# A decoder's first layer norm: order across tiles, a two-tensor normalise, first loads and value products reordered, one weight's low part on VectorE

## The reference

```python
def _layernorm(x, axis=-1, eps=1e-05):
    m = jnp.mean(x, axis=axis, keepdims=True)
    v = jnp.var(x, axis=axis, keepdims=True)
    return (x - m) / jnp.sqrt(v + eps)
...
x = x + _L0_attn_ref(_layernorm(x, axis=-1), L0_attn_Wq, L0_attn_bq, L0_attn_Wk, L0_attn_bk, L0_attn_Wv, L0_attn_bv, ...)
```

## Time and profile before

| | |
|---|---|
| median of 3 runs | 1648.77 us (1647.23 to 1651.67) |
| the profiled execution | 1647.46 us |
| its span in the trace | 1645.7 us |
| PE busy | 1584.0 us, 96% of the span |
| DVE, ACT, POOL busy | 57%, 45%, 40% |
| chain that ended last | PE 84%, DVE 7%, ACT 4%, issue 4%, POOL 1% |
| granted TensorE clock, mean | 0.996 |

### The profile page before, as it was taken

How to read it: one execution, slowest core, us unless ns; L and a number is a source line. 1 busy time by engine, 2 the same in 40 slices (tenths; PEclk the granted TensorE clock), 3 DMA queues, 4 the chain that set the end, 5 groups by cost and what they waited for, 6 DMA issues and landing times.

```text
span 1645.7 us, 24561 instructions
## 1 busy us (share of the span) xinstructions
PE 1584.0 (96%) x9832; PEld 1347.7 (82%) x9832; DVE 937.4 (57%) x1531; ACT 732.5 (45%) x1231; POOL 665.3 (40%) x483
## 2 busy tenths in 40 slices
PE   7999999989999999989999989998989999999998
PEld 7898666878899998768889976876768888888887
DVE  6555664366545455587758667353666455554554
ACT  3113655322587765666511156333545334353342
POOL 3875542440498873421127634112432422212221
PEclk9999999999999999999999999999999999999999
DMA  4110003123222007200002100110011111111111
GB/s 167 52 65 28 2 2 117 56 84 126 97 89 65 14 1 268 93 1 1 1 8 70 52 27 1 50 39 26 21 33 39 49 61 52 45 50 47 53 57 45
DMA packets 28580, 88.52 MB, mean 54 GB/s; under 512 B 4154, under 2 KB 4282, under 8 KB 28215
## 3 DMA queue, kind: packets, MB, share of 16 engines
q1 hardware_dynamic: 28468, 86.96, 15.3%
HBM read 85.11 MB, written 1.84 MB: 53 GB/s over the span
## 4 chain that ended last, share of the span: by engine, by line
PE 84%; DVE 7%; ACT 4%; issue 4%; POOL 1%; ACTq 0%; DVEq 0%; POOLq 0%
PE PS L261 19%; PE PS L263 18%; PE PS L262 18%; PE PS L266 7%; PE PS L1125 4%; PE PS L1462 3%; PE PS L1477 2%; PE PS L561 2%; PE PS L952 1%; PE PS L585 1%; PE PS L1709 1%; PE PS L1697 1%; PE PS L551 1%; PE PS L569 1%; DVE xn L326 1%
## 5 line engine op out<-in xcount | busy, mean ns | idle before, releaser
L307 POOL TENSOR_TENSOR HL<-stg,HL 128x1024 fp32r<-128x1024 f32 (+2 forms) x111 | 243.7, 2197 | 510.1 <-ACT HL L302 492.0
L261 PE MATMUL PS<-XT,HL 128*128 128x448 f32 x608 | 224.7, 370 | 2.9 <-DVE XT L342 2.2
L263 PE MATMUL PS<-XT,HL 128*128 128x448 f32 x608 | 222.6, 366 | 0.0
L262 PE MATMUL PS<-XT,HL 128*128 128x448 f32 x608 | 222.6, 366 | 0.0
L302 ACT ACTIVATE HL<-stg 128x1024 fp32r<-128x1024 f32 (+2 forms) x111 | 104.5, 944 | 215.0 <-PE PS L263 199.2
L261 PE MATMUL PS<-HL,XT 128*128 128x512 f32 (+1 forms) x380 | 137.2, 361 | 2.0 <-POOL HL L307 1.2
L263 PE MATMUL PS<-HL,XT 128*128 128x512 f32 (+1 forms) x380 | 134.2, 353 | 0.0
L262 PE MATMUL PS<-HL,XT 128*128 128x512 f32 (+1 forms) x380 | 134.1, 353 | 0.0
L261 PEld LDWEIGHTS PS<-XT,HL 128*128 128x128 f32 x608 | 114.5, 188 | 15.6 <-DVE XT L342 3.3
L262 PEld LDWEIGHTS PS<-XT,HL 128*128 128x128 f32 x608 | 114.5, 188 | 9.6
L263 PEld LDWEIGHTS PS<-XT,HL 128*128 128x128 f32 x608 | 114.3, 188 | 9.6
(11 more groups left out here) (314 smaller groups left out, 3805.2 us busy)
## 6 DMA issues: line engine op xcount, KB each, us to landing
stg<-in_wst SPq DMA_DIRECT2D x87, 512.0 KB, 3.2
stg<-in_wst SPq DMA_DIRECT2D x16, 352.0 KB, 3.0
stg<-in_wst SPq DMA_DIRECT2D x16, 320.0 KB, 3.0
wsum<-in_wfc SPq DMA_DIRECT2D x8, 512.0 KB, 3.6
wsum<-in_wpj SPq DMA_DIRECT2D x8, 512.0 KB, 3.5
raw<-in_wfc SPq DMA_DIRECT2D x8, 512.0 KB, 6.3
stg<-in_wst SPq DMA_DIRECT2D x16, 256.0 KB, 2.5
raw<-in_wpj SPq DMA_DIRECT2D x7, 512.0 KB, 7.0
```

Source lines behind the costliest of these rows:

```text
L261: e.matmul(out, lh, rh, start=start, stop=False)
L262: e.matmul(out, lh, rl, start=False, stop=False)
L263: return e.matmul(out, ll, rh, start=False, stop=stop)
L307: e.tensor_tensor(slot(k)[:, 1, 0:n], stg[k % NSTG][:, 0:n], slot(k)[:, 0, 0:n].bitcast(F), A.subtract).then_inc(*done("pool_w", k))
```

## The change

The first layer norm no longer calls `ln_front`. Statistics (`stats`) and normalising (`norm`) are separate steps, so that statistics of two tiles can stand next to each other, and the last step of `norm` is a `scalar_tensor_tensor` whose second tensor is the reciprocal root broadcast over 512 columns. ScalarE's list, PE's list and the order of the first DMAs are rearranged to match. The low part of weight piece 0 (`low_part`, `rest_w(e, 0)`) moves from POOL to VectorE. Warm-up products are 10, 4 and 5 in place of 10 and 8; the last nine multiply the identity in place of the zeros. Turns 4 and 5 stand between value groups, and turn 6 behind unit 0.

```diff
--- before.py
+++ after.py
@@ -289,10 +289,13 @@
         def load(e, k):
             n = width(k)
             if k >= NSTG:
-                e.wait_ge(*(upon("pool_w", k - NSTG) if k - NSTG in cut_no else upon(*freed[k - NSTG])))
+                e.wait_ge(*(upon(*low_part(k - NSTG)) if k - NSTG in cut_no else upon(*freed[k - NSTG])))
                 if order[k - NSTG][0] == "kq" and order[k - NSTG][1] % 2 == 0:
                     e.wait_ge(*upon("dve_q", "K", order[k - NSTG][1] // 2))
             e.dma_start(stg[k % NSTG][:, 0:n], g["wst"][where[order[k]], :, 0:n]).then_inc(*landed(f"sp_stg{k % NSTG}", k))
+
+        def low_part(k):
+            return ("pool_w", k) if k else ("dve_w", k)
 
         def round_w(e, k):
             n = width(k)
@@ -305,10 +308,10 @@
             n = width(k)
             e.wait_ge(*upon("act_w", k))
             e.tensor_tensor(slot(k)[:, 1, 0:n], stg[k % NSTG][:, 0:n], slot(k)[:, 0, 0:n].bitcast(F),
-                            A.subtract).then_inc(*done("pool_w", k))
+                            A.subtract).then_inc(*done(*low_part(k)))
 
         def has_w(e, k):
-            e.wait_ge(*upon("pool_w", k))
+            e.wait_ge(*upon(*low_part(k)))
             return slot(k)
 
 
@@ -355,22 +358,27 @@
                 return last
 
             e.wait_ge(*upon("dve_p0", "blank"))
-            blank(10)
+            def blank2(n):
+                for i in range(n):
+                    e.matmul(PS[:, 3, 0:128], C("ident"), C("ident"), start=True, stop=True)
+
+            blank(10).then_inc(*done("pe_p0", "blank"))
             e.wait_ge(*upon("sp_ident"))
             ln_turn(e, "x", 0, xn[0], 4)
-            blank(8).then_inc(*done("pe_p0", "blank"))
+            blank2(4)
             ln_turn(e, "x", 1, xn[1], 5)
-            for b, vh in ((0, 0), (1, 0)):
-                e.wait_ge(*upon("dve_ln", "x", b, "lo"))
-                value0(e, b, vh)
-            ln_turn(e, "x", 2, xn[0], 6)
-            value0(e, 0, 1)
-            value0(e, 1, 1)
-            ln_turn(e, "x", 3, xn[1], 7)
-            for b in (2, 3):
+            blank2(5)
+            for b in range(2):
                 e.wait_ge(*upon("dve_ln", "x", b, "lo"))
                 value0(e, b, 0)
+            for b in range(2):
+                ln_turn(e, "x", 2 + b, xn[b], 6 + b)
                 value0(e, b, 1)
+            for vh in range(2):
+                for b in range(2, 4):
+                    e.wait_ge(*upon("dve_ln", "x", b, "lo"))
+                    value0(e, b, vh)
+                ln_turn(e, "x", 4 + vh, xn[vh], 4 + vh)
             for u, (kind, i, half) in enumerate(units0):
                 w = slot(piece[kind, i][0])
                 if u < 2 or (u > 3 and half == 0):
@@ -387,10 +395,8 @@
                     last.then_inc(*done("pe_p0", u, ab))
                 if half == 1:
                     freed[piece[kind, i][0]] = "pe_p0", u, 1
-                if u < 2:
-                    for t in range(4 + 2 * u, 6 + u):
-                        e.wait_ge(*upon("dve_ln", "x", t - 4, "lo"))
-                        ln_turn(e, "x", t, xn[t % 2], t)
+                if u == 0:
+                    ln_turn(e, "x", 6, xn[0], 6)
             for b in (4, 5):
                 e.wait_ge(*upon("dve_p0", 18, b - 4))
                 for vh in range(2):
@@ -415,20 +421,23 @@
             e.wait_ge(*upon("dve_p0", "eps", 2))
             e.activation(rs[:, 1, 1:2], eps[:, 0:1], ACT.Sqrt)
             ln_root(e, "x", 0)
+            ln_root(e, "x", 1)
             ln_hi(e, "x", 0, 4)
             round_w(e, 0)
-            ln_root(e, "x", 1)
             ln_hi(e, "x", 1, 5)
-            for t in range(2, 4):
-                round_w(e, t - 1)
-                ln_root(e, "x", t)
-                ln_hi(e, "x", t, 4 + t)
+            round_w(e, 1)
+            ln_root(e, "x", 2)
+            ln_root(e, "x", 3)
+            ln_hi(e, "x", 2, 6)
+            ln_hi(e, "x", 3, 7)
+            round_w(e, 2)
+            ln_root(e, "x", 4)
+            ln_root(e, "x", 5)
+            ln_hi(e, "x", 4, 4)
             round_w(e, 3)
-            for i in range(2):
-                for t in range(4 + 2 * i, 6 + i):
-                    ln_root(e, "x", t)
-                for t in range(4 + 2 * i, 6 + i):
-                    ln_hi(e, "x", t, t)
+            ln_root(e, "x", 6)
+            ln_hi(e, "x", 5, 5)
+            ln_hi(e, "x", 6, 6)
             for k in (4, 5, 6):
                 round_w(e, k)
             for k in range(7, 15):
@@ -454,27 +463,55 @@
             for i, v in enumerate((1e-5, 1e-6, 1e-11)):
                 e.memset(eps[:, i:i + 1], v).then_inc(*done("dve_p0", "eps", i))
             e.memset(xn[1][:, 0:128], 0.0).then_inc(*done("dve_p0", "blank"))
-            for t in range(4):
+
+            def stats(t):
                 e.wait_ge(*upon(f"sp_x{t}"))
-                ln_front(e, "x", t, xn[t % 2][:, :], (None, ("pe_p0", "blank"), ("pe_ln", "x", 0), ("pe_ln", "x", 1))[t])
-                if t < 3:
-                    ln_lo(e, "x", t, 4 + t)
+                k = t % 2
+                e.bn_stats(st6[:, k, 0, :], x[:, t, :]).then_inc(*done("dve_ln", "x", t, "st"))
+                e.wait_ge(*upon("dve_ln", "x", t, "st"))
+                e.bn_aggr(mv[:, k, :], st6[:, k, 0:1, :].rearrange("p a c -> p (a c)")).then_inc(*done("dve_ln", "x", t, "mv"))
+
+            def norm(t):
+                k = t % 2
+                e.wait_ge(*upon("act_ln", "x", t, "root"))
+                e.reciprocal(rs[:, k, 2:3], rs[:, k, 1:2]).then_inc(*done("dve_ln", "x", t, "rstd"))
+                if t:
+                    e.wait_ge(*(upon("pe_ln", "x", t - 2) if t > 1 else upon("pe_p0", "blank")))
+                e.wait_ge(*upon("dve_ln", "x", t, "rstd"))
+                e.scalar_tensor_tensor(out=xn[k][:, :], in0=x[:, t, :], scalar=mv[:, k, 0:1], in1=rs[:, k, 2:3].to_broadcast([P, D]),
+                                       op0=A.subtract, op1=A.mult).then_inc(*done("dve_ln", "x", t, "xn"))
+
+            stats(0)
+            norm(0)
+            stats(1)
+            norm(1)
+            ln_lo(e, "x", 0, 4)
+            rest_w(e, 0)
+            ln_lo(e, "x", 1, 5)
+            stats(2)
+            stats(3)
+            norm(2)
+            norm(3)
+            ln_lo(e, "x", 2, 6)
+            ln_lo(e, "x", 3, 7)
+            stats(4)
+            stats(5)
+            norm(4)
+            norm(5)
             e.wait_ge(*upon("sp_bv"))
             value0_out(e, 0)
-            ln_lo(e, "x", 3, 7)
             value0_out(e, 1)
-            for u in range(2):
-                for t in range(4 + 2 * u, 6 + u):
-                    e.wait_ge(*upon(f"sp_x{t}"))
-                    ln_front(e, "x", t, xn[t % 2][:, :], ("pe_ln", "x", t - 2))
-                    if t < 6:
-                        value0_out(e, t - 2)
-                if u == 0:
-                    e.wait_ge(*upon("sp_sml"))
-                    e.wait_ge(*upon("sp_cst"))
-                rope0(e, u)
-                for t in range(4 + 2 * u, 6 + u):
-                    ln_lo(e, "x", t, t)
+            stats(6)
+            ln_lo(e, "x", 4, 4)
+            value0_out(e, 2)
+            norm(6)
+            value0_out(e, 3)
+            ln_lo(e, "x", 5, 5)
+            e.wait_ge(*upon("sp_sml"))
+            e.wait_ge(*upon("sp_cst"))
+            rope0(e, 0)
+            ln_lo(e, "x", 6, 6)
+            rope0(e, 1)
             rope0(e, 2)
             rope0(e, 3)
             e.tensor_scalar(M("sinks", S), M("sinks", S), 8.0, None, A.mult).then_inc(*done("dve_p0", "sinks8"))
@@ -501,7 +538,7 @@
                 e.wait_ge(*upon("dve_p0", u, 1))
                 e.tensor_tensor(outs[1], u2, u3, A.add).then_inc(*done("pool_p0", u, 1))
 
-            for k in range(4):
+            for k in range(1, 4):
                 rest_w(e, k)
             for u in range(3):
                 sums(u)
@@ -2542,18 +2579,19 @@
 
             rows(0)
             e.dma_start(cst[:, 0:P], g["cst"][:, 0:P]).then_inc(*landed("sp_ident"))
+            rows(1)
             load(e, 0)
-            rows(1)
             load(e, 1)
             rows(2)
-            e.dma_start(bv[:, :], g["bob"][:, 1, :]).then_inc(*landed("sp_bv"))
             rows(3)
             load(e, 2)
+            rows(4)
+            e.dma_start(bv[:, :], g["bob"][:, 1, :]).then_inc(*landed("sp_bv"))
+            rows(5)
+            rows(6)
+            load(e, 3)
             e.dma_start(cst[:, P:], g["cst"][:, P:]).then_inc(*landed("sp_cst"))
             e.dma_start(sml[:, :], g["sml"]).then_inc(*landed("sp_sml"))
-            load(e, 3)
-            for t in range(4, NT):
-                rows(t)
             load(e, 4)
             e.dma_start(bo[0:S, :], g["bob"][:, 0, :]).then_inc(*landed("sp_bob", "first"))
             e.dma_start(bo[S:P, :], g["bob"][0:P - S, 0, :]).then_inc(*landed("sp_bob"))
```

## The result

| | before | after |
|---|---|---|
| median, 4 runs each | 1648.05 us (1647.23 to 1651.67) | 1638.79 us (1637.46 to 1640.28) |
| profiled execution, its span | 1647.46, 1645.7 | 1637.46, 1635.6 |

The ratio is 0.9938, 95% interval 0.9925 to 0.9951: 9.3 us between the medians, 10.0 between the two profiled executions. The forecast was 7.4 us faster, 1641.4 us; the time lies in the range, near its fast end. The gain is about a quarter larger than forecast, and the rest of the document is about where that quarter comes from.

What follows compares the result with a forecast made beforehand. One core's PE, busy 96% of 1645.7 us, bounds the kernel, so only its waits or slow work can be won; 7.4 us gained at unit 2, carried to the end, takes 1648.77 to 1641.4 us, range 1638.0 to 1646.0.

Steps and rivals of the forecast that it cites:

- The chain: First stage: predicted starts of turn 1, first value product, units 0, 1, 2 and fifth unit; 7.4 us gained at unit 2.
- Loads: Start DMAs: x1 moved ahead of first weight lands at 5.1, weight at 7.3; other moves priced at nothing.
- Rival A: Start DMAs: loads bring nothing, x1 still lands at 7.6; gain 5.5 us, 1643.3; chance 0.12.
- Normalise: VectorE: two-tensor form takes 0.75 free, 0.20 more per tile than 0.55, and still queues behind POOL.
- E: VectorE normalise: the new form frees it from POOL; gain 8.0 us, 1640.7; chance 0.06.
- B: VectorE normalise: half rate with two non-bf16 SBUF sources, 1.28 each; gain 5.3 us, 1643.5; chance 0.05.
- Low part on VectorE: First weight's subtraction of 1024 columns takes VectorE 1.22; 2.34 leaves POOL.
- A start moved there is therefore kept by what follows: Behind 52.00 PE is busy without a gap, so the 7.4 us gain carries to the end.
- The sum: Gain taken at unit 2's start, 41.39 before and 34.00 after: 7.4 us, carried to the end.
- C: Later half-clock stretches, as at 1115 to 1123, give back 3.4 of 7.4 us; gain 4.0, 1644.8; chance 0.12.
- the sign itself: Stated sign of a wrong forecast: fifth unit's start at 44.6 comes true and the end doesn't follow.
- D: Warm-up: PE's clock rise is missed and PE stays at 1.2 GHz; 8.9 us slower, 1657.7; chance 0.05.

Runs made afterwards that it cites:

- after_wait: Changed kernel with tile 6's low part behind the rope of unit 1 on VectorE instead of ahead; median 1643.12 us, ratio 0.997 to the kernel before.
- fill_late: Kernel before plus 11 unread identity products ahead of and behind turn 6 only; 1646.72 us against 1647.99, ratio 0.9989.
- 7 products: Kernel before with 7 warm-up products in the second batch in place of 8, profiled twice; 1651.72 us the second time.

## Why the prediction came out as it did

*The waits:* right. The chain gave 8.02, 9.78, 23.87, 29.14, 34.00 and 44.6 against 8.07, 9.90, 24.23, 29.52, 34.47 and 44.99, and 7.4 at unit 2 against 6.9. The links are up to 0.5 late, mostly from normalises held longer than taken: 1.22 for tile 2 (0.92 taken) and 1.48 for tile 4 (1.23).

*Loads:* 5.1 taken, 5.7 measured for x1, but VectorE was free only then; 7.3 and 7.0 for the weight. Rival A falls; undoing the move puts tile 1 back by 1.6.

*Normalise:* 0.75 as taken, held by GpSimd as taken; E falls. B falls too: 512 columns on 128 partitions, with both sources float32 in SBUF, take the same time as on 24. The Trainium skill, Vector Engine (DVE) Microarchitecture Reference, section 7, has it at half, which this case's 0.75 doesn't bear out.

*Low part on VectorE:* 1.22 as worked out.

*Failed: "A start moved there is therefore kept by what follows", the 7.4 carried to the end as it stands.* The sum took a removed wait to be worth its length. What a wait costs beyond that was put at nothing, without a reason, and the one rival at this step, C, could only take something off. The prediction named the sign itself: the start at 44.6 comes true and the end doesn't follow. It came within 0.4, and the end lies 3.0 us beyond it in the profiled pair. The runs show in its place that TensorE's wait ahead of unit 2 costs more than its length. With it went the wider spacing of units 4 to 19, 1.5 us, and, in part of the executions, 3.4 or 6.8 us at half speed, which make the way from unit 2 to unit 4 1.6 or 2.7 us longer. after_wait puts a wait of 2.0 back and pays 4.3 to 4.7; fill_late leaves unit 4 where it was and gets 1.3 us back. So the 9.3 between the medians are 7.0 and a remainder of 2.3, of the size that after_wait shows (2.3 to 2.7) and that filling the waits gave (2.1).

*Failed: the ground given against D,* that an idle 2.55 did not bring the clock down. It did not in the one profile at hand; it did in the next one of the same kernel, and in three more kernels near 12 us. D itself didn't come (full clock from 4 up to 731 us in the changed kernel). C's place near 1115 gave 1.5 us in the profiled pair; that the medians have any of it is not shown.

*Open:* what sets the spacing. Seven of eight profiles with a wait of 2 us ahead of unit 2 show 0.2067, all ten without it 0.2027. That the wait brings it is shown in both directions (fill_late, after_wait); by what mechanism isn't, nor why one execution escaped it. It does not begin directly behind the wait: in the first profile of the kernel before, units 2 and 3 still run at 0.2027, and 0.2067 begins with unit 4. Half clock over units 2 and 3 is not the link either, since it came with both spacings (7 products, twice).

## What to carry to other kernels

When TensorE's wait of 2 us or more goes away, look for more than its length: compare the granted clock and the start-to-start spacing of the instructions behind it, in more than one profile. Where the wait can't go, products nobody reads can fill it; here that delayed nothing (unit 4 at 51.80 against 52.00). And a normalise held by GpSimd isn't freed by a form with two SBUF inputs; put work beside GpSimd that reads PSUM, or statistics, as the new order does. In the changed kernel a low part at 23.37 (0.66) and a value read-out at 23.94 (0.68), both with one input in PSUM, ran beside GpSimd's subtraction from 22.88 to 25.28 and took no longer than elsewhere.

## What the hardware showed that was not expected

- TensorE's spacing for 448 columns has two values at full granted clock, 0.2027 and 0.2067, and keeps one from unit 4 to unit 19, over 70 us.
- Half-speed stretches come behind waits of 2.0 to 2.8 us in some executions and not in others of the same kernel: none, one or both of those near 12 and 41 in the profiles with the old order, ten of sixteen such places in all. The one near 12 cost the old order 0.1 us at unit 0, where waits of 1.3 and 1.5 us lie behind it, and the new order with the old loads 0.7 us at turn 2. The Trainium skill, TensorE: Matmul & The Clock Gate, section "HAM oscillation — how this bites in real kernels", puts the danger with longer idle gaps; here 1.97 was enough once, so the measurement decides.
- A normalise with two SBUF inputs and statistics on VectorE differ: the statistics at 10.27 and 11.09 ran beside GpSimd's subtraction from 10.39 to 12.79 unhindered (0.69 and 0.66), the normalise at 12.12 did not (1.22).
